# A graph attention layer on one core: adjacency turned at other steps, the masks' order on VectorE changed, compares moved to ScalarE, prologue and last rows reordered

## What is computed

```
A_tilde = adj + eye(n);  mask = A_tilde > 0
Wh = (x @ W.T).reshape(n, 4, 32)
score_l = einsum('nhd,hd->nh', Wh, a_l);  score_r = einsum('nhd,hd->nh', Wh, a_r)
e = score_l[:, :, None] + score_r.T[None, :, :]
e = where(e >= 0, e, 0.2 * e);  e = where(mask[:, None, :], e, -inf)
alpha = softmax(e, axis=2)
out = elu(einsum('nhm,mhd->nhd', alpha, Wh).reshape(n, 128))
y = layernorm(x + out)
```

## Time and profile before

| | |
|---|---|
| runs | 1816.73, 1818.39, 1822.62 us; median 1818.39 |
| the profiled execution's own time | 1823.02 us |
| its span, first to last instruction | 1821.2 us |
| VectorE (DVE) busy | 1734.2 us, 95% |
| TensorE matmul (PE) busy; weight load (PEld) | 1659.8 us, 91%; 1627.4 us, 89% |
| ScalarE (ACT) busy | 1612.2 us, 89% |
| GpSimd (POOL) busy | 24.0 us |
| DMA | 368.12 MB, mean 202 GB/s |
| granted TensorE clock, mean | 0.986 of full speed (2.4 GHz) |

### The profile page before, as it was taken

One profiled execution on the slowest core, in us unless ns is written; L12 is line 12 of the kernel. 1 busy time (PEld: TensorE's weight loads), 2 busy tenths in 40 slices (PEclk: granted clock), 3 DMA queues, 4 the chain that ended last, 5 costly groups with the idle time before them and its releaser, 6 DMA issues. The chain is left out here.

```text
span 1821.2 us, 81366 instructions
## 1 busy us (share of the span) xinstructions
PE 1659.8 (91%) x37067; PEld 1627.4 (89%) x37067; DVE 1734.2 (95%) x1928; ACT 1612.2 (89%) x1217; POOL 24.0 (1%) x34
## 2 busy tenths in 40 slices
PE   6788888889898999999999999999999899999993
PEld 6787887889898999999999999999999899999893
DVE  5999999988988999999999999999999999999996
ACT  4989999789779998998989998998989998998981
POOL 0000000000000100000000100000000100000000
PEclk9899999999999999999999999999999999999997
DMA  8995898999997676576666676666662131121111
GB/s 256 342 341 195 308 311 297 367 334 354 355 323 253 208 241 217 181 237 198 216 211 207 200 238 200 211 209 205 220 194 59 31 95 43 36 57 36 32 36 31
DMA packets 241478, 368.12 MB, mean 202 GB/s; under 512 B 12912, under 2 KB 103408, under 8 KB 239600
## 3 DMA queue, kind: packets, MB, share of 16 engines
q1 hardware_dynamic: 241136, 362.92, 60.7%
HBM read 345.57 MB, written 17.30 MB: 199 GB/s over the span
## 5 line engine op out<-in xcount | busy, mean ns | idle before, releaser
L488 ACT ACTIVATE bmask<-lrow,rtab 128x2048 fp8e4<-128x2048 f32 (+1 forms) x936 | 1483.2, 1661 | 33.1 <-DVE cmask L700 24.1
L396 PE MATMUL psum<-vring,bmask 128*128 128x99 bf16 x14336 | 723.4, 208 | 35.5 <-DVE bmask L695 13.2
L396 PE MATMUL psum<-vring,cmask 128*128 128x99 bf16 x14336 | 718.9, 208 | 37.1 <-DVE cmask L700 21.8
L396 PEld LDWEIGHTS psum<-vring,bmask 128*128 128x128 fp8e4 x14336 | 669.0, 97 | 44.8 <-issue 30.6
L396 PEld LDWEIGHTS psum<-vring,cmask 128*128 128x128 fp8e4 x14336 | 661.6, 98 | 51.9 <-DVE cmask L700 30.7
L700 DVE SCALAR_TENSOR_TENSOR cmask<-acache,bmask 128x1024 int32<-128x1024 int32 x512 | 625.0, 1221 | 27.5 <-PE psum L396 20.6
L695 DVE SCALAR_TENSOR_TENSOR bmask<-acache,bmask 128x1024 int32<-128x1024 int32 x512 | 624.2, 1219 | 0.0
L682 DVE TENSOR_SCALAR bmask<-lrow,rtab 128x2048 fp8e4<-128x2048 f32 (+1 forms) x344 | 357.6, 1055 | 0.0
L457 ACT CAST acache<-trp 128x512 int16<-128x512 f32 x128 | 74.0, 578 | 111.4 <-PE trp L364 111.1
L364 PE MATMUL trp<-pack,abuf 128*128 128x64 bf16 x4096 | 144.1, 194 | 15.9 <-issue 11.1
L364 PEld LDWEIGHTS trp<-pack,abuf 128*128 128x128 bf16 x4096 | 132.8, 99 | 17.6 <-issue 12.3
(11 more groups left out here) (62 smaller groups left out, 259.9 us busy)
## 6 DMA issues: line engine op xcount, KB each, us to landing
abuf<-in_adj_dram SPq DMA_DIRECT2D x256, 1024.0 KB, 8.4
vring<-v_scratch SPq DMA_DIRECT2D x384, 99.0 KB, 3.1
lrow<-l_scratch SPq DMA_DIRECT2D x16, 1024.0 KB, 7.8
v_scratch<-vt SPq DMA_DIRECT2D x16, 792.0 KB, 11.1
vring<-v_scratch SPq DMA_DIRECT2D x64, 198.0 KB, 8.2
cmask<-in_x_dram SPq DMA_DIRECT2D x16, 256.0 KB, 4.4
late<-in_x_dram SPq DMA_DIRECT2D x16, 256.0 KB, 4.2
out_dram<-late SPq DMA_DIRECT2D x16, 256.0 KB, 3.5
```

The costliest lines, as they stand in the source:

```text
L396: return nc.tensor.matmul(psum[:, bank, at * S3:(at + 1) * S3], mask[:, j * P:(j + 1) * P], values, start=opening, stop=True, skip_group_c ...
L488: last = nc.scalar.activation(to, rows, ACT.Relu, bias=rtab[:, 2 * s + i, H + h:H + h + 1], scale=BIG, saturate=False)
```

## The change

- **Turning times.** `turned_at` after pass 0 goes by `LATER_TURNS`: 48 blocks, one in 2.4 steps, in passes 1 to 4, then 64 blocks, one in 3.9 steps, from step 148 (pass 4) to step 393 (pass 12). Blocks per pass before: 14, 16, 16, 16, then 8 in each of passes 4 to 11. Now: 14, 14, 13, 13, 12, 8, 8, 8, 8, 9, 8, 8, 3.
- **Compares.** Those on VectorE per pass, before and now: pass 0: 40 and 33; pass 1: 26 and 26; passes 2 and 3: 40 and 35 each; passes 4, 8, 12: 15 and 13; the other wide passes: 17 and 15. The steps that hold none on VectorE are spread (10, 17, 22, 29 instead of 13, 24).
- **Masks.** The loop on VectorE now does `mask_b(q + 1)`, `compare(q + 2)`, `mask_c(q)`. `mask_b` waits for its block only in the first step that uses it, and for the diagonal's OR where its block holds one; `add_diagonal` comes at other steps of passes 4, 8, 12.
- **Prologue.** `xs` has six buffers (all of `cmask`); the first two blocks' transfers stand behind more of x; the scores' way through DRAM begins earlier for chunk 0; `rtab` is made in two parts; block 0 is turned after the loop over x; ScalarE does all four compares of step 0 within that loop; the four copies of `copy_l` on ScalarE become one; `mask_b(0)` and `mask_c(0)` stand ahead of `weigh(1)`.
- **End.** The last chunk's rows are finished in two halves: weights times sums, ELU, residual, statistics, power; ScalarE normalises the first eight rows of 128, VectorE the other eight, and SP stores each half after its own.

```diff
+    LATER_TURNS = [STEPS + n * 12 // 5 for n in range(3 * QUADS)] + [148 + n * 39 // 10 for n in range(NB - 4 * QUADS)]
     def turned_at(q):
         if q < STEPS:
             return [FIRST_TURNS[q]] if q in FIRST_TURNS else []
-        if q < 4 * STEPS:
-            return [] if q % 2 else [QUADS + (q - STEPS) // 2]
-        n = 4 * QUADS + (q - 4 * STEPS) // 4
-        return [n] if q % 4 == 1 and n < NB else []
+        return [n for n in range(QUADS, NB) if LATER_TURNS[n - QUADS] == q]
...
         if w == 0:
-            return 2 if s % 2 == 0 else 1
+            return 0 if s < 2 else 2 if s % 2 == 0 and s % 8 != 6 else 1
         if w == 1:
             return 0 if s < 6 else (2 if s % 3 == 0 else 1)
         if narrow(w):
-            return 0 if s < 5 else 2
-        return 0 if s < 6 or s in (13, 24) or (w % 4 == 0 and s in (8, 9)) else 1
+            return 0 if s < 5 else 1 if s % 5 == 0 else 2
+        return 0 if s < 6 or s in (10, 17, 22, 29) or (w % 4 == 0 and s in (8, 9)) else 1
...
-    BR, CR, VR, VS, AH = 6, 3, 4, 3, 3
+    BR, CR, VR, VS, XS, AH = 6, 3, 4, 3, 6, 3
...
             for g in range(XG):
                 load_x(g)
-                if g in (5, 8, 11, 14):
-                    load_block((g - 5) // 6, [(g - 5) // 3 % 2])
-            store_l(0)
-            sp.wait_ge(l_stored, 16)
-            load_lrow(0)
+                if g in (8, 11, 14, 15):
+                    k = (8, 11, 14, 15).index(g)
+                    load_block(k // 2, [k % 2])
+                if g == 11:
+                    store_l(0)
+                if g == 13:
+                    sp.wait_ge(l_stored, 16)
+                    load_lrow(0)
...
             for g in range(XG):
                 copy_wh(g)
-                if g > 4 and g % 4 == 2:
-                    copy_l(g // 4 - 1)
                 if g == 13:
-                    evacuate(0)
+                    compare(0)
...
-            copy_l(NC - 1)
+            evacuate(0)
             evacuate(1)
-            compare(0)
             highest(0)
+            copy_l()
+            middle(0)
             compare(1)
-            middle(0)
             compare(2)
             highest(1)
...
             weigh(0)
-            rest(0)
             add_diagonal(0, 0)
             add_diagonal(0, 1)
+            rest(0)
             compare(0)
+            mask_b(0)
             lowest(0)
+            compare(1)
+            mask_c(0)
             weigh(1)
             for q in range(Q):
                 w, s = WHERE[q]
-                mask_b(q)
+                if q + 1 < Q:
+                    mask_b(q + 1)
...
-                if q + 1 < Q:
-                    compare(q + 1)
-                mask_c(q)
+                if q + 2 < Q:
+                    compare(q + 2)
+                if q > 0:
+                    mask_c(q)
...
+            e = len(FINISHED) - 2
+            weigh_sums(w, 0)
+            add_halves(w, 0)
+            lower(w, 0)
+            weigh_sums(w, 1)
+            residual(w, 0)
+            add_halves(w, 1)
+            add_exp(w, 0)
+            lower(w, 1)
             statistics(e, FINISHED[e][1])
+            residual(w, 1)
             moments(e)
+            add_exp(w, 1)
+            statistics(e + 1, FINISHED[e + 1][1])
+            moments(e + 1)
             mean_part(e)
+            mean_part(e + 1)
+            dve.wait_ge(nmr_done, e + 2)
+            for j in FINISHED[e + 1][1]:
+                nc.vector.tensor_scalar(zz[:, j], zz[:, j], vrs[:, j:j + 1], nmr[:, j:j + 1], ALU.mult, ALU.add).then_inc(last_rows, 1)
```

153 lines of the change are left out of this document (88 added, 65 removed).

## The result

The changed kernel takes **1793.35 us** (median of 4 runs, 1787.99 to 1793.88), the kernel before on the same chip 1820.36. The ratio is 0.983, with a 95% interval of 0.981 to 0.985: 27 us faster, not 59. It lies above the range of the prediction, 1743 to 1781. The profiled execution took 1793.73 us for a span of 1791.9.

A forecast was written before the change was run, and what follows sets the result against it. Bounds named: VectorE and ScalarE in passes 0 and 1, transfers in 2 and 3, VectorE from 4 on. Terms -4, -26.9, -6.7, -9.0, -5.5, -2.4, -4.6 sum to -59.1, giving 1759.3 us; range 1743 to 1781.

The forecast's parts named there:

- The bound of passes 5 to 11: Passes 5 to 11: VectorE is full; moving two wide compares takes 2.4 us a pass off it, ScalarE gains 3.8.
- Passes 4 to 7: Passes 4 to 7: the bound moves from VectorE to ScalarE, mostly in pass 4; 416.7 becomes 410 us, -6.7.
- Passes 8 to 11: Passes 8 to 11: two wide compares a pass move to ScalarE; 415.8 becomes 406.8 us, -9.0.
- Passes 2 and 3: Passes 2 and 3: spread adjacency and five narrow compares a pass moved; 246.9 becomes 220 us, -26.9.
- Rival A: Passes 2 and 3 end at 236 instead of 220, V's transfers still meeting adjacency's; total 1775 us, chance 0.12.
- Rival E: Passes 2 and 3 did not wait for adjacency transfers; total 1779 us, chance 0.13 shared with rival B.
- Start and first passes: Prologue, passes 0 and 1: first product at 43 instead of 51.43; pass 2 starts 4 us earlier, bounds 0 and 9.
- It is not kept: Prologue: the earlier first product is mostly lost, since blocks 2 to 5 can start only 3 to 4 us earlier.
- The order at nothing: VectorE's loop: putting the AND a step ahead of the XOR costs and saves nothing.
- Passes 12 to 15: Two wide compares a pass moved to ScalarE: -5.5 us in passes 12 to 14, -2.4 in pass 15.
- rivals B and D: ScalarE's waits for turned blocks: B, half stay, 1775 to 1778 us (0.13 with Rival E); D, all stay, 1837 (0.03).
- The end: Tail of pass 15: finishing in halves makes the chain 14.7 instead of 18.05 us, two stores fewer behind it; -4.6.

The follow-up runs named there:

- g3: g1 with the wide compares of passes 4 to 11 back at the old split, the move to ScalarE kept from pass 12 on: 1789.49 us.
- g4: The changed kernel with 8 transposes instead of 32 for each turned block from block 64 on, so less TensorE work: 1767.86 us.
- experiment 13: g1 with a block's two adjacency transfers issued in two successive steps from pass 1 on, same bytes: 1781.47 us.
- g1: The changed kernel with the edits of f1 and f3 together: 1782.99 us.
- f1: The changed kernel with the 64 blocks after the first 64 turned every fourth step from step 149, instead of one in 3.9 steps: 1788.01 us.
- f3: The changed kernel with all of x issued before SP's wait for stored row scores, scores' rows and block 1 loaded behind x: 1792.02 us.
- e3: The changed kernel with the old turning table put back: 1802.48 us.
- e4: The kernel before with the new turning table alone: 1814.17 us.
- f4: The changed kernel with each block's second transfer cut from four tile rows to one from block 16 on, 3/8 of adjacency bytes left out: 1773.90 us.
- h2: The kernel before with only the AND of step q+1 put ahead of the XOR of step q: 1821.78 us.
- e1: The changed kernel with VectorE's old loop order of AND(q), compare(q+1), XOR(q): 1794.75 us.
- e2: The changed kernel with the two moved wide compares a pass back on VectorE: 1805.61 us.

## Why the prediction was wrong, point by point

The direction was right, and of seven terms the last three were met or beaten. Four missed, by 1 us (start), 12.6 (passes 2 and 3), 3.8 (4 to 7) and 12.1 (8 to 11), by the prediction's own cut.

- **The bound of passes 5 to 11 was the step that failed.** The sum took 2.4 us a pass off VectorE as the only full engine, and put the next bound at ScalarE (405.0 and 401.3 us for four passes), with TensorE below it (399.6 and 396.8). For one of the passes 5 to 7 its prices give TensorE 32 x 2.86 + 8 x 0.93 = 99.0 us of the 101.9. In the trace TensorE's own start-to-start times make 99.3, and stops and waits over 0.12 us another 2.6, of which 2.1 lie in the first third of the pass, where VectorE still works on the last pass's sums and weights. Those the sum left out. So two engines were the bound at once before, and taking work from one gave 0.9 us a pass (g3) instead of 2.4. g4 shows the other side: with 5.6 us less of TensorE a pass, passes 5 to 7 fall to 98 to 100. VectorE's idle time in the earlier trace rows named it full; it did not say that TensorE was not.
- **Passes 4 to 7: +4.7 (-2.9 by the prediction's cut) instead of -6.7.** Pass 4 went from 103.1 to 108.8: four blocks more are 3.7 us of TensorE, its stops within groups (experiment 13) went from 2.0 to 5.1, and its waits ahead of groups fell by 1.1. The sum did count the blocks, but against ScalarE as the bound. ScalarE is busy 106.33 of 108.8 there, yet g3, which takes the moved compares off it in this pass, takes 109.2 against g1's 109.0. That speaks for a ScalarE that is full beside the bound; one execution of each is all there is.
- **Passes 8 to 11: +2.4 (+3.1) instead of -9.0.** Besides the bound, 6.7 us were the table's 3.9-step rhythm (f1, and 7.4 between f3 and g1). Of these, 4.0 lie in pass 8: a load of V that landed behind four stores and a block, a wait of 2.7 us, and 1.25 us of lower clock. No term of the prediction had this. The rest lies in passes 9 and 10, and its cause was not found. With f1's table the stretch takes 411.3, 4.3 us less than before; what is still missing to the forecast is of the size of TensorE's stops in four passes, and was not taken apart.
- **Passes 2 and 3: -19.0 (-14.3) instead of -26.9.** The mechanism was right (e3, e4: the table alone gives 18 us of TensorE's 19), the size off. By the prediction's own cut the passes took 232.6 us instead of 220. The term mis-sized is the transfers' floor of 209: the DMA engines were busy 0.94 of 232.6, 219 us, for 72.9 MB instead of 71.2, at 332 GB/s while busy instead of 340. So the transfers led the next engine by 8 us where the sum had VectorE in front, and what stands above them is 13 us of waits where I took 8. Rival A had the nearest number, 236, with a chance of 0.12. Its mechanism, V meeting the adjacency, shows in one wait of 1.9 us in these passes. Rival E falls with e3 and e4. f4, with transfers out of the way, leaves 6.5 us above VectorE's floor, near the 8 that I took for waits.
- **Start and first passes: -0.3 (-2.9) instead of -4.** The first product came at 49.6 instead of 43. TensorE waited 5.8 us for the last groups of x, which stood behind SP's wait for stored scores and a transfer of 1 MB; f3 takes 3.8 us of this away. "It is not kept" was wrong as well: with f3's edit the first product and the start of pass 2 both come 3.7 us earlier. That passes 0 and 1 take 1.5 us more than before is within what versions with the same code differ by (258.9 to 260.9 in f3, g1 and g3).
- **The order at nothing:** right in the total alone (h2), wrong in its reason. "Where VectorE is full, order saves no time" fails: where it is full the order gave 1.5 to 1.7 us a pass (h2, e1). An XOR right behind the AND that it reads starts 1.25 us after it, one that reads an older AND 1.14 (medians of 11 and 12 in pass 13, before and h2). With the 11 such pairs of the kernel before this makes 1.4 of the 1.5 us, and with e1's 13 pairs 1.6 of 1.7.
- **Passes 12 to 15: -10.8 (-5.3 and a share of -7.0) instead of -7.9, in part by luck.** Passes 13 to 15 lost 3.9 us each where 2.4 was forecast: 2.4 by the compares (e2) and 1.5 by the order, which the sum had at nothing. Pass 12 got 0.8 us longer. That the term was met is two misses of opposite sign.
- **Coupling through ScalarE (rivals B and D):** did not come. Its waits for turned blocks halved, 23.9 to 12.2 us, as the prediction expected of "lead, not need". The other half of the worry did: VectorE's AND waits 44.7 us for ScalarE's compares, the sign named as one of error. It cost little: with the wide compares taken off ScalarE again (e2, g3) no stretch of passes 4 to 11 got shorter.
- **The rule on where to compute.** "ScalarE: Activation LUTs", Rules for kernel authors, in the Trainium skill would have had the compares stay on VectorE. In passes 13 to 15 the trace disagrees with its outcome: 98.0 against 100.4 us (e2). VectorE is busy all of pass 13 there and ScalarE, with the moved compares, 96.6 of 98.1. In passes 4 to 11 the move is worth 0.9 us a pass (g3), and no pass is longer with it. The prediction called rival D the rule's way, but D was priced by ScalarE's waits for turned blocks and not by the 17 us worked out from the rule.
- **The end: -6.3 instead of -4.6.** The chain was drawn through GpSimd's two powers in series. At 1.64 us each they are not: GpSimd waits 0.66 us for the second half's moments, which set the chain up to there.

The end of the changed kernel, answering to the earlier trace rows (its timeline):

```profile
1774.37 0.69 DVE L779 TENSOR_TENSOR late<-acc,wgt 128x512 f32<-128x512 f32 x1
...
1780.53 1.64 POOL L948 TENSOR_TENSOR vrs<-vrs,epsc 128x8 f32<-128x8 f32 x1
...
1782.82 0.20 POOL L946 TENSOR_TENSOR vrs<-mv,epsc 128x8 f32<-128x8 f32 x1 [0.66 <-DVE mv L824]
1782.83 3.18 ACT L505 ACTIVATE late<-late,nmr,vrs 128x128 f32<-128x128 f32 x8 [4.73 <-DVE nmr L830]
1783.11 1.64 POOL L948 TENSOR_TENSOR vrs<-vrs,epsc 128x8 f32<-128x8 f32 x1
1784.77 0.17 DVE L830 SCALAR_TENSOR_TENSOR nmr<-mv,vrs 128x8 f32<-128x8 f32 x1 [1.98 <-POOL vrs L948]
1784.98 2.14 DVE L921 TENSOR_SCALAR late<-late,vrs,nmr 128x128 f32<-128x128 f32 x8
1786.04 2.71 SPq L273 DMA_DIRECT2D out_dram<-late  x4
```

The power of 8 columns takes 1.64 us where 16 took 2.91 at the end before; I had taken 3.2 for it. (Elsewhere in the changed kernel, with VectorE busy beside it, the same instruction took up to 4.83, so the columns alone don't set it.) Eight normalisations take 2.14 us on VectorE, where I had 1.7. From the weighed sums to the end of the last normalisation (1784.98 + 2.14) it is 12.75 us, against 18.05 before and 14.7 predicted.

## What to carry to other kernels

Before work is taken off the engine that looks full, add up each other engine's work and the waits that it has at the start of each pass. If that sum is the pass's length too, two engines bound it, and relieving one gives little. When a table of issues is changed, look at what then stands directly ahead of each small load: here stores and a block in front of one load of V cost 4 us. On an engine that is full, the order of independent and dependent instructions is worth measuring: here it moved 1.5 to 3 us in 100. And name the noise of a stage from versions that share its code before reading 2 us into it.
